# One-hots of the last 16 aggregation steps divided between ScalarE and GpSimd in a graph-attention kernel

## What is computed

```python
h = maximum(layernorm(x), 0)                  # 6250 x 256
xm = h @ W_n2m.T                              # 128 channels
ea = edge_attr @ W_r2m.T                      # 206250 edges, 32 numbers each
xl, xr = xm @ Wl.T + bl, xm @ Wr.T + br
u = leaky_relu(xl[src] + xr[dst] + ea @ We.T, 0.2)
logits = einsum('ehd,hd->eh', u, att)
alpha = softmax over the edges of one dst(logits)
out = segment_sum(xl[src] * alpha, dst) + bias   # and one self loop for each node
return x + out @ W_m2n.T
```

## Time and profile before

| | us |
|---|---|
| median of three runs | 2429.84 |
| the three runs | 2429.38, 2429.84, 2435.47 |
| profiled execution, its own time | 2429.01 |
| span of its instructions | 2426.8 |
| prologue, up to | about 130 |
| last front half (relu of step 426) | 2286.2 |
| drain, up to the last `acc` addition | 2334.73 |
| finale | 2335.0 to the end |

### The profile page before, as it was taken

The page is one execution under the profiler, slowest core; times in us unless marked ns, Lnnn a source line. Parts: engine busy times, 40 slices in busy tenths (PEclk is TensorE's granted clock), DMA queues, the critical chain, the costliest instruction groups (busy, mean ns, idle before and its releaser), DMA issues. The chain is left out here.

```text
span 2426.8 us, 71198 instructions
## 1 busy us (share of the span) xinstructions
PE 2250.9 (93%) x16556; PEld 1731.1 (71%) x16557; DVE 1483.2 (61%) x4174; ACT 1438.3 (59%) x4331; POOL 1721.3 (71%) x1914
## 2 busy tenths in 40 slices
PE   3968999999999999999999999999999999999977
PEld 2745777777777777777777777777677777777756
DVE  4734666656665666566656665666566656666676
ACT  2714666656665666566656666666566656666653
POOL 3777777777777777777777777777777777777401
PEclk9989999999999999999999999999999999999999
DMA  6243443444444444444444444444444334444117
GB/s 199 80 109 96 103 104 97 98 100 107 98 99 102 106 98 99 102 104 99 100 101 105 99 100 101 106 99 99 100 104 99 100 100 106 99 99 98 45 51 123
DMA packets 288519, 244.84 MB, mean 101 GB/s; under 512 B 168503, under 2 KB 259608, under 8 KB 287826
## 3 DMA queue, kind: packets, MB, share of 16 engines
q1 hardware_dynamic: 221726, 116.00, 21.1%
q0 software_dynamic: 60704, 120.20, 19.8%
q10 hardware_dynamic: 5652, 3.68, 0.5%
HBM read 228.23 MB, written 19.40 MB: 102 GB/s over the span
## 5 line engine op out<-in xcount | busy, mean ns | idle before, releaser
L778 POOL DMA_INDIRECT xl_g<-xl_table,src_tab x1708 | 1636.2, 958 | 522.9 <-issue 514.4
L999 DVE SCALAR_TENSOR_TENSOR uT<-banks,relu 128x256 f32<-128x256 f32 x854 | 347.3, 422 | 536.6 <-issue 513.4
L860 PE MATMUL banks<-msg,onehot 128*128 128x177 f32 x3416 | 634.4, 328 | 7.2 <-DVE acc L955 2.9
L860 PEld LDWEIGHTS banks<-msg,onehot 128*128 128x128 f32 x3416 | 518.7, 191 | 170.8 <-issue 153.6
L898 ACT ACTIVATE distance<-iota_n,minus_slot 128x128 f32<-128x128 f32 x1708 | 541.1, 390 | 0.0
L813 PE MATMUL banks<-ident,xl_g 128*128 128x128 f32 x3416 | 464.3, 280 | 31.4 <-DMA xl_g<-xl_table,src_tab 31.3
L813 PEld LDWEIGHTS banks<-ident,xl_g 128*128 128x128 f32 x3416 | 445.4, 202 | 37.9 <-DMA xl_g<-xl_table,src_tab 37.8
L913 ACT ACTIVATE relu<-banks 128x256 f32<-128x256 f32 x854 | 315.8, 383 | 144.2 <-PE banks L813 115.8
L794 PE MATMUL banks<-onehotT,xr_parts 128*128 128x256 bf16 x2562 | 355.8, 275 | 22.5 <-issue 17.3
L903 ACT ACTIVATE onehot<-distance 128x512 f32<-128x512 f32 x427 | 269.0, 630 | 116.8 <-PE banks L860 105.3
L907 ACT ACTIVATE rbfT<-banks 128x128 f32<-128x128 f32 x427 | 116.5, 273 | 352.9 <-PE banks L808 347.4
(11 more groups left out here) (193 smaller groups left out, 1643.5 us busy)
## 6 DMA issues: line engine op xcount, KB each, us to landing
slot_bc<-slot_dram SPq DMA_DIRECT2D x427, 128.0 KB
xl_g<-xl_table,src_tab POOLq DMA_INDIRECT x1708
rbf<-in_edge_attr SPq DMA_DIRECT2D x854, 32.0 KB
masks<-masks_dram SPq DMA_DIRECT2D x864, 12.1 KB
out<-in_x SPq DMA_DIRECT2D x16, 336.0 KB
out<-result POOLq DMA_DIRECT2D x6, 896.0 KB, 9.3
xl_table<-lr_sb SPq DMA_DIRECT2D x49, 64.0 KB, 1.5
xl_in<-xl_table SPq DMA_DIRECT2D x7, 448.0 KB, 4.9
```

The source lines that it names most:

```text
L778: pool.indirect_dma_start(out=xl_g[:, k % RING, t], out_offset=None, in_=xl_table, in_offset=bass.IndirectOffsetOnAxis(ap=src_tab[:, e:e + ...
L860: mm = nc.tensor.matmul(U_ps[h], onehot[:, j % 2, t], msg[:, j % 2, t], start=i == 0, stop=i == PT - 1)
L999: nc.vector.scalar_tensor_tensor(out=uT[:, s % 2, h * PIECE:(h + 1) * PIECE], in0=z_ps[h], scalar=SLOPE, in1=relu[:, h], op0=ALU.mult, op1 ...
```

## The change

From step 411 on (`DRAIN`), ScalarE makes only tiles 0 and 1 of a step's one-hot: two distances in place of four, and one ReLU over 256 columns in place of 512. GpSimd makes tiles 2 and 3, straight into `onehot`, each in one two-operation `tensor_scalar` (add the negated slot to the node numbers, compare with 0). These 32 instructions stand behind its last gather. Each pair waits for the aggregation of step m - 2; the first also for ScalarE's one-hot of step 410. TensorE's aggregation of these steps waits for one more semaphore, `drain_ready`.

```diff
+        DRAIN, OURS = STEPS - LAG + 1, TILES // 2
...
+            for m in range(DRAIN, STEPS):
+                pool.wait_ge(agg_done, TICK * (m - 1))
+                if m == DRAIN:
+                    pool.wait_ge(oh_ready, TICK * DRAIN)
+                for t in range(OURS, TILES):
+                    nc.gpsimd.tensor_scalar(onehot[:, m % 2, t], iota_n[:], minus_slot[:, one(TILES * m + t)], 0.0,
+                                            ALU.add, ALU.is_equal).then_inc(drain_ready, 1)
...
                     pe.wait_ge(oh_ready, TICK * (k - LAG + 1))
+                    if isinstance(k, int) and k - LAG >= DRAIN:
+                        pe.wait_ge(drain_ready, (TILES - OURS) * (k - LAG - DRAIN + 1))
...
-                    for t in range(TILES):
+                    late = max(0, k - LAG + 2 - DRAIN) if isinstance(k, int) else 0
+                    tiles = OURS if late else TILES
+                    for t in range(tiles):
                         nc.scalar.activation(distance[:, t], iota_n[:], ACT.Abs,
                                              bias=minus_slot[:, one(TILES * (k - LAG + 1) + t)]).then_inc(dist_ready, 1)
-                    act.wait_ge(dist_ready, TILES * (k - LAG + 2))
+                    act.wait_ge(dist_ready, TILES * (k - LAG + 2) - (TILES - OURS) * late)
                     if inside(k - LAG - 1, STEPS):
                         act.wait_ge(agg_done, TICK * (k - LAG))
-                    nc.scalar.activation(onehot[:, m % 2], distance[:], ACT.Relu, scale=-1.0, bias=1.0
+                    nc.scalar.activation(onehot[:, m % 2, 0:tiles], distance[:, 0:tiles], ACT.Relu, scale=-1.0, bias=1.0
                                          ).then_inc(oh_ready, TICK)
```

More of the change, by code:

```diff
@@ L712, in edge_loop @@
          ends_listed, fall_ready, shrink_ready, back_done, ends_ready, firsts_raised, run_ready, below_ready,
-         last_ready, weight_ready, wT_done, spread_done, factor_ready, rescaled, x_set) = map(sem, (
+         last_ready, weight_ready, wT_done, spread_done, factor_ready, rescaled, x_set, drain_ready) = map(sem, (
              "set_up", "acc_zero", "ohT_ready", "node_saved", "rbfT_done", "rbfT_ready", "z_done", "relu_ready", "u_ready", "L_done",
@@ L717, in edge_loop @@
              "back_done", "ends_ready", "firsts_raised", "run_ready", "below_ready", "last_ready", "weight_ready",
-             "wT_done", "spread_done", "factor_ready", "rescaled", "x_set"))
+             "wT_done", "spread_done", "factor_ready", "rescaled", "x_set", "drain_ready"))
         XPARTS = 16
         XPART = (FBATCH - 1) * FB * P // XPARTS
+        DRAIN, OURS = STEPS - LAG + 1, TILES // 2
         block = ctx.enter_context(nc.Block())
```

## The result

The changed kernel took 2438.04 us (median of eleven runs; 2434.64 to 2443.65), the kernel before, run beside it, 2432.88 us (2429.38 to 2437.21). All ratios compare fast runs with fast runs, so that one run of `e11_share_12_again` at 5276.91 us and one of the kernel before beside it at 3739.24 are left out. The changed kernel is slower by a quarter of a per cent, less than the 0.3% that the prediction took for the least that can be told, but clearly not the 2428.3 us that it forecast. The profiled execution took 2437.86 us (span 2435.7), 8.9 us more than the span of before.

A forecast was written before the change was run, and what follows sets the result against it. The drain was taken as a chain passing between engines, with ACT the bound in its last steps. -1.96 us gained there plus 0.5 for contention gave -1.5, so 2429.84 - 1.5 = 2428.3 us, range 2424.5 to 2432.5.

The forecast's parts named there:

- The step that failed: At the block's end: the finale's memsets on GpSimd wait for nothing new, counted at no cost.
- Rival 5: GpSimd's branch could be reached late if its last gathers were late, so the change would not act; given no chance.
- ScalarE's step: In the drain's last steps, ACT's time per step falls from 2.08 to 1.25 us with two distances and half a one-hot.
- The last stretch: Last steps up to the last addition: gain of 1.96 us, with VectorE limiting the aggregations instead of ScalarE.
- GpSimd's tile: One-hot tile on GpSimd: 0.55 us each, 1.1 the pair, hidden by the 1.44 us aggregation; cost 0, range 0 to +0.5.
- Contention: In the drain, GpSimd's computing slows VectorE's 11 two-input operations: +0.5 us, between 0 and 3.2.
- The rest at 0: First drain steps and both CHAIN to TURN stretches hang on VectorE, PE and semaphores; gain 0, also taken behind the earlier SCALE.
- a sign of slack in VectorE: ENDS of the last batch stays at 2310.7; a move by a microsecond would show VectorE had the slack denied it.
- The clock, rival 2: Batch chains: shifting the drain can move PE's falls to 1.2 GHz, worth 3.9 us; 2424.4 or about 2429.7; chance 0.1.
- The chance for "slower": Whole kernel slower by over 0.3%: 0.06, from GpSimd becoming the bound plus a little for two of three runs being high.
- GpSimd in every step: In the drain, slow GpSimd tiles become the bound, TensorE waiting at L871 each step: 15.4 us more, 2445; chance 0.05.

The follow-up runs named there:

- e11_share_12_again: Changed kernel with GpSimd sharing one-hots only in steps 411 to 422, ScalarE making all four tiles from 423 on, timed again; ratio to the kernel before 1.0001 [0.9975, 1.0027].
- e8_late_wait_425: Kernel before plus a bare GpSimd wait for the aggregation of step 425 behind its last gather, no computing there; ratio 1.0020 [0.9996, 1.0045].
- e10_late_wait_again: Kernel before plus a bare GpSimd wait for the aggregation of step 425 behind its last gather, same code timed again; ratio 1.0007 [0.9979, 1.0034].

## Why the prediction was wrong

**The step that failed** is a single sentence: "The finale's memsets on GpSimd come after the block's end and wait for nothing new." They wait for the closing DRAIN, and so does every engine at the barrier. The rows stood on record, though the lists of GpSimd's instructions ahead of the prediction show L663 as a branch alone, without its DRAIN: the earlier trace rows has the MEMSET released by `POOLq L663`, after 51.42 us. I read it as idle time of an engine with nothing to do, and never asked how long what stands under that name takes. One more view of the trace of before, the rows of L663, shows 23.34 us for GpSimd's DRAIN, an end 8.2 us after the last gather, and less than 1.5 us for all other engines'. Rival 5 had the right question (what if GpSimd comes late?) but asked it of the branch's beginning, not of its end. Priced with that row and the last one-hot of the changed kernel: 2332.3 + 8.2 = 2340.5, six behind the last addition.

**ScalarE's step: right, a little short.** Forecast 2.08 to 1.25 us; measured 1.28. The half one-hot took 0.42, not 0.38, and the two distances 0.68, as expected (0.39 + 0.29).

**The last stretch: right, over by 0.2.** Forecast -1.96 us, VectorE then binding. Measured -1.75 (8.62 to 6.87), the same within 0.01 in all seven profiles that share from 411 or 413 to the end. The last two aggregations wait for VectorE, as said; that of 424 still waits 0.38 us for ScalarE.

**GpSimd's tile: mis-sized.** 0.55 us estimated, 0.717 measured, between the bounds 0.29 and 0.93. The pair of 1.41 us still fits beside the aggregation of 1.44, but only just, so the term was rightly 0. One operation of 256 columns at 0.93 was a poor basis for halving: two operations on 128 columns cost more than half of it (0.717 against 0.465); whether the second operation or the fixed part is to blame was not tried.

**Contention: +0.5 us that did not come, and on the other engine.** VectorE's two-input operations kept their length within 0.03 us. GpSimd's tiles stretched:

```profile
2303.64 0.41 DVE L1060 SCALAR_TENSOR_TENSOR last_max<-masks,run_max 128x256 f32<-128x256 bf16 x1
2303.65 1.68 POOL L788 TENSOR_SCALAR onehot<-iota_n,minus_slot 128x128 f32<-128x128 f32 x2 [1.00 <-PE banks L871]
```

1.68 instead of 1.41 us for the pair that begins 0.01 us after a two-input operation of 0.41, and 0.988 us for the longest single tile. The rule of the Trainium skill (SBUF — State Buffer, § Who interferes with whom) that the two exclude each other would have held GpSimd back by 0.40 us here; it lost 0.27. The price for VectorE that I drew from the rule, near the whole gain, did not come. Nor did it depend on who began first by the trace: pairs that began 0.03 and 0.05 us ahead of a two-input operation (2310.17 and 2324.29) grew too, to 1.53 and 1.65 us, while VectorE kept its 0.31 and 0.41, and where L1067 at 2330.10 fell within GpSimd's pair of 2329.06 neither grew.

**The rest at 0: right at equal clock.** The earlier two parts of the drain went from 17.17 and 21.41 us to 16.06 and 20.70, more than 0. A second profile of the same kernel has 17.19 and 21.37. The granted clock in the first part was 0.80 before and in the second profile, and 0.89 in the first one: this 1.1 us went with the clock, not with the change. The 0.7 us of the second part, at 0.92 in all three, has no explanation here. ENDS of the last batch moved with the first part (2312.93, 1.1 earlier than before if counted from the last `uT`). The prediction had called such a move a sign of slack in VectorE; but counted from the first of the two `factor`s, ENDS came 5.99 us behind it before and 6.03 after, so it was not that. Of the 3.6 us by which the drain was shorter, 1.75 come from the change and the rest was luck with this profile.

**The clock, rival 2.** Its falls in the batch chains did shift, by about the size it gave. Its place in the finale I did not see: 2.3 us in the profiled execution, behind the idle time of the gap. The granted clock in the finale's opening was 0.50 to 0.64 in the seven profiles with a gap of 4 us or more, and 0.71 to 1.00 in the seven without. But this is not a fixed price of the gap: the opening took between 5.96 and 7.46 us in the profiles with it, and between 5.09 and 6.55 in those without.

**Sum and spread.** -1.75 + 6.0 = +4.3 us follows from terms that repeat in both profiles of the changed kernel. The medians say +5.2 and +8.0; the slower opening of the finale (+2.3 and +1.7) accounts for part of the rest. The chance for "slower" was put at 0.06 on a mechanism (GpSimd in every step) that did not happen. What was missing was the cost of ending an engine's part of a block late.

## What to carry to other kernels

When a change gives an idle engine work at the end of a block, price the block's end as well: look up that engine's DRAIN in the trace of before, see how long after its last instruction it ended, and add that to the new last instruction. GpSimd, having issued many indirect gathers, may owe microseconds there; pay them early with a DRAIN of its own while nobody waits, and check that the first instruction behind it isn't needed sooner. An idle row released by the engine's own queue is not an empty one.

## What the runs showed of the hardware

- GpSimd's DRAIN with indirect gathers since the last DRAIN ends late: 7.6 to 9.2 us behind the last instruction with 128 gathers and more, 1.9 us with 8, 2.9 with 32, 5.3 with 64. With 1708 gathers it took 8.2 us also 80 us after the last of them. Without a gather or a transfer issued by GpSimd since the last DRAIN it ended within 0.2 us of the last instruction (in the prologue 0.7, with eight indirect loads more than 70 us back). Why is open.
- A GpSimd `tensor_scalar` of two operations on 128 x 128 f32 took 0.717 us; when it met a two-input VectorE operation and either grew, it was GpSimd's (to 0.988), not VectorE's.
- The unchanged kernel took 2430 us on some chips and 3700 on others, at a granted clock near 0.85 instead of 0.98 over the span, the difference lying in the loop; with a bare wait behind the gathers (`e8_late_wait_425`, `e10_late_wait_again`), the three parts of the drain there were within 0.3 us of those on a 2430-us chip, at the same granted clocks. The cause was not looked for.
